# A two-layer graph network on one core: the copy into the accumulator moves to ACT's queue, gathers lose their pacing, and dense rows get a schedule of their own

## The reference

```
h  = relu(layernorm(x))
# stage one (per edge, all its inputs from the node table at dst)
gate  = silu(edge_attr @ W1.T + b1) @ W2.T + b2 + q[type[src], type[dst]]
msg   = gate * h[dst] * cutoff(dist) * node_vec[dst]
agg   = segment_sum(msg, src) / segment_sum(node_vec[dst], src)
x     = x + layernorm(h + agg) * gamma + beta
# stage two
h  = relu(layernorm(x))
m  = (relu(h @ Wr1[rel] + b) @ Wr2[rel])[src] * norm
x  = x + relu(segment_sum(m, dst) + bias2)
```

## Time and profile before

| what | us |
|---|---|
| median of three runs (lowest, highest) | 1523.17 (1517.62, 1532.58) |
| profiled execution, first to last instruction | 1526.4 |
| TensorE, VectorE, ScalarE, GpSimd busy | 1130.4, 1319.3, 668.1, 1026.1 |
| last message of stage one written / last add of stage one issued / first gather of stage two | 687.0 / 740.0 / 743.5 |

### The profile page before, as it was taken

One profiled execution on the slowest core, in us unless ns is written; L12 is line 12 of the kernel. 1 busy time (PEld: TensorE's weight loads), 2 busy tenths in 40 slices (PEclk: granted clock), 3 DMA queues, 4 the chain that ended last, 5 costly groups with the idle time before them and its releaser, 6 DMA issues.

```text
span 1526.4 us, 20418 instructions
## 1 busy us (share of the span) xinstructions
PE 1130.4 (74%) x5198; PEld 831.4 (54%) x5198; DVE 1319.3 (86%) x3932; ACT 668.1 (44%) x1627; POOL 1026.1 (67%) x809
## 2 busy tenths in 40 slices
PE   5889899989999899881068888887878887775000
PEld 2767677777777777771035555555555555554000
DVE  6999999999989998980289999998989899888599
ACT  2444444544445444540155555555555555554000
POOL 7655667777877787566667787877777777766000
PEclk9666655655556655655575656655565556666555
DMA  7999986666666656642445666555555555554899
GB/s 225 307 324 327 328 236 157 153 146 143 142 166 149 149 139 143 155 101 11 100 120 143 166 167 156 140 138 137 136 139 127 132 131 138 138 127 81 328 400 398
DMA packets 154391, 268.73 MB, mean 176 GB/s; under 512 B 73818, under 2 KB 90411, under 8 KB 153380
## 3 DMA queue, kind: packets, MB, share of 16 engines
q1 hardware_dynamic: 78228, 223.53, 43.8%
q0 software_dynamic: 68992, 24.64, 18.5%
q10 hardware_dynamic: 7056, 19.27, 3.1%
HBM read 194.33 MB, written 112.55 MB: 201 GB/s over the span
## 4 chain that ended last, share of the span: by engine, by line
PE 34%; DVE 20%; DMA 19%; POOL 12%; issue 10%; ACT 3%; SPq 1%; POOLq 0%; DVEq 0%; ACTq 0%
PE ps_m L572 10%; POOL agg L485 8%; DMA t<-agg,src_all 6%; PE ps_m L661 6%; PE ps_qs L572 6%; DMA lows<-low 4%; PE ps_k L647 3%; DVE same L858 2%; DMA agg<-y,once 2%; DMA agg<-ysq,once 2%; DVE t L1074 2%; DVE x L1070 2%; PE ps_k L559 2%; PE ps_k L560 2%; PE ps_qs L610 1%
## 5 line engine op out<-in xcount | busy, mean ns | idle before, releaser
L521 POOL DMA_INDIRECT agg<-sums,once x196 | 312.7, 1595 | 103.5 <-issue 79.8
L443 POOL DMA_INDIRECT nodes<-in_table,dst_all x196 | 194.9, 995 | 102.2 <-issue 51.7
L512 POOL DMA_INDIRECT t<-agg,src_all x196 | 191.5, 977 | 66.1 <-issue 53.9
L572 PEld LDWEIGHTS ps_m<-msg,same 128*128 128x128 f32 x980 | 200.8, 314 | 29.0 <-issue 29.0
L572 PE MATMUL ps_m<-msg,same 128*128 128x48 f32 x980 | 208.5, 398 | 1.0 <-issue 1.0
L647 PE MATMUL ps_k<-h_t,rw_sb 56*128 56x256 f32 x588 | 122.7, 536 | 114.0 <-ACT hid L742 91.3
L572 PEld LDWEIGHTS ps_qs<-msg,same 128*128 128x128 f32 x980 | 183.6, 289 | 2.1 <-DVE msg L950 2.1
L572 PE MATMUL ps_qs<-msg,same 128*128 128x49 f32 x980 | 180.7, 363 | 2.0 <-DVE msg L950 2.0
L485 POOL DMA_INDIRECT agg<-x,once x84 | 137.4, 1635 | 43.9 <-issue 21.7
L647 PEld LDWEIGHTS ps_k<-h_t,rw_sb 56*128 56x128 f32 x588 | 62.9, 242 | 157.1 <-ACT hid L742 115.2
L559 PE MATMUL ps_k<-types_lo,low_hot 128*128 128x392 bf16 x196 | 95.7, 488 | 52.7 <-DVE low_hot L833 51.0
(11 more groups left out here) (149 smaller groups left out, 2620.2 us busy)
## 6 DMA issues: line engine op xcount, KB each, us to landing
agg<-in_both SPq DMA_DIRECT2D x14, 2758.0 KB, 15.3
t<-agg SPq DMA_DIRECT2D x49, 784.0 KB, 5.3
kept<-kept_out SPq DMA_DIRECT2D x49, 404.0 KB
kept_in<-kept SPq DMA_DIRECT2D x49, 404.0 KB, 3.5
agg<-bias_rows SPq DMA_DIRECT2D x49, 384.0 KB
out<-t ACTq DMA_DIRECT2D x49, 384.0 KB, 5.8
rows<-in_src_rows SPq DMA_DIRECT2D x49, 256.0 KB, 4.2
rows<-in_dst_rows SPq DMA_DIRECT2D x49, 256.0 KB, 3.2
```

Source lines behind the costliest of these rows:

```text
L443: pool.indirect_dma_start(nodes[s][:, t, :], None, table, bass.IndirectOffsetOnAxis(ap=dst_all[:, c:c + 1], axis=0)).then_inc(nodes_in[b % ...
L512: pool.indirect_dma_start(t2[b % T2S][:, t, :], None, wide, bass.IndirectOffsetOnAxis(ap=src_all[:, c:c + 1], axis=0)).then_inc(ends_in[b ...
L521: pool.indirect_dma_start(agg1, bass.IndirectOffsetOnAxis(ap=once1[b % LAG1][:, t:t + 1], axis=0), sums1[b % LAG1][:, t, :], None, compute ...
L572: last = mm(ps[:, t * width:(t + 1) * width], kept_same[:, at:at + P], m[:, v, :], start=(v == t), stop=(v == TILES - 1))
```

## The change

In stage one: (1) ACT issues all fourteen copies into `agg0` before anything else, as soon as the two index arrays are in. (2) POOL gathers the first 26 blocks with no waits, then waits for the copies; from then on two gathers follow each block's adds, as before. (3) Chunks are taken apart from edge blocks. Blocks 0 to 12 have none; block 13 begins chunks 0 and 1; blocks 14 to 48 each finish one or two (21 with one, 14 with two) and begin the one two ahead. A second chunk of a block stands on VectorE behind the last `type_of`, ahead of the message. (4) The type table holds two types in a number, so a lookup has 196 columns in place of 392 and `type_of` reads 196; two small shift and mask instructions unpack it. (5) The destination's one-hot: VectorE copies four numbers to bf16, TensorE spreads them with four bf16 matmuls of 128 columns, and ScalarE makes the one-hot with Square and Relu. (6) Square roots for edges and chunks are separate. (7) `keep_clock` adds bf16 matmuls of 512 columns whose result nobody reads: nine in a block and one for each chunk.

```diff
-PRERUN = FIRST + 2 * STEPS
+PRERUN = 26
+def dense_steps():
+    steps = [[] for _ in range(NBLOCK)]
+    steps[DENSE0 - 1] = [(None, 0), (None, 1)]
+    c = 0
+    for b in range(DENSE0, NBLOCK):
+        while c * (NBLOCK - DENSE0) < (b + 1 - DENSE0) * NBLOCK:
+            steps[b].append((c, c + 2 if c + 2 < NBLOCK else None))
+            c += 1
...
-                if b < FILLS:
-                    sp.dma_start(fill_to[b], fill_from[b]).then_inc(S["wide_set"], 16)
...
-            for b in range(1, FIRST):
+            for b in range(1, PRERUN):
                 gather(b)
-            for step in range(STEPS):
-                pool.wait_ge(S["onehot_done"], step + 1)
-                gather(FIRST + 2 * step)
-                pool.wait_ge(S["pc_done"], step + 1)
-                gather(FIRST + 2 * step + 1)
             pool.wait_ge(S["wide_set"], 16 * FILLS)
...
+            def keep_clock(ps, n):
+                for _ in range(n):
+                    mm(ps, ident_bf[:, :], spin, start=True, stop=True)
...
             for b in range(NBLOCK):
+                keep_clock(ps_idle, 3)
                 if b + 1 < NBLOCK:
                     lookup(b + 1, 0)
                     lookup(b + 1, 1)
-                pe.wait_ge(S["onehot_done"], b + 1)
-                need(pe, S["onehot_t_done"], b)
+                keep_clock(ps_idle, 1)
+                pe.wait_ge(S["zd_done"], b + 1)
+                need(pe, S["apart_done"], b)
                 for t in range(TILES):
-                    last = nc.tensor.transpose(ps_t[0:NTYPE, t * P:(t + 1) * P], onehot[:, t, :], ident[:, :])
-                last.then_inc(S["turned_t_done"], 1)
+                    last = mm(ps_t[:, t * P:(t + 1) * P], zd_bf[:, t:t + 1].to_broadcast([P, P]), ident_bf[:, :], start=True, stop=True)
+                last.then_inc(S["zd_wide_done"], 1)
...
                 last.then_inc(S["gate_done"], 1)
+                keep_clock(ps_idle, 1)
                 if b + 1 < NBLOCK:
                     h1(b + 1)
-                    centred(b + 1)
+                    keep_clock(ps_idle, 1)
+                for done, begun in steps[b]:
+                    if begun is not None:
+                        centred(begun)
+                        keep_clock(ps_idle, 1)
...
+            act.wait_ge(S["idx_in"], 32)
+            for f in range(FILLS):
+                act.dma_start(fill_to[f], fill_from[f]).then_inc(S["wide_set"], 16)
...
-                nc.scalar.copy(onehot_t[:, :], ps_t[0:NTYPE, :]).then_inc(S["onehot_t_done"], 1)
+                A(apart[:, :], ps_t[0:NTYPE, :], ACT.Square, bias=minus_type[:, :]).then_inc(S["apart_done"], 1)
+                act.wait_ge(S["apart_done"], b + 1)
+                A(onehot_t[:, :], apart[:, :], ACT.Relu, scale=-1.0, bias=1.0).then_inc(S["onehot_t_done"], 1)
...
+                for done, begun in steps[b][1:]:
+                    if begun is not None:
+                        dense_sum(begun)
+                    if done is not None:
+                        dense_var(done)
+                        dense_rsum(done)
+                    if begun is not None:
+                        dense_centre(begun)
+                    if done is not None:
+                        dense_keep(done)
```

More of the change, by code:

```diff
@@ L74, with rooted_at @@
 WIN = place(TILES)
+def dense_steps():
[6 more added lines that the diff above has]
+            c += 1
+    assert c == NBLOCK and max(len(s) for s in steps) == 2
+    return steps
+def rooted_at(steps, b):
+    return [s[0] for s in (steps[b - 1][1:] if b > 0 else []) + (steps[b][0:1] if b < NBLOCK else []) if s[0] is not None]
 def build(nc, table, both, xt_in_dram, xn_in_dram, types, edge_src, edge_dst, src_rows, dst_rows, edge_feat, dist, norm, rel,
@@ L250, in build @@
         ps_c = ps_k[0]
-        ps_l = [ps_k[1][:, a, 0:NHI] for a in range(2)]
+        ps_l = [ps_k[1][:, a, 0:NPK] for a in range(2)]
         ps_h1 = ps_m[0:H, :]
+        ps_idle = ps_k[0][:, 1, :]
         ps_gate = ps_s[:, BE // 2:BE // 2 + TILES * H]
@@ L319, in load_xt, with store_kept @@
                 sp.dma_start(xn[c % 2][:, :], xn_in_dram[c]).then_inc(xn_in[c % 2], 16)
+            def store_kept(b):
+                for c in rooted_at(steps, b):
+                    sp.wait_ge(S["std_d_done"], c + 1)
+                    sp.wait_ge(S["pc_done"], c + 1)
+                    sp.dma_start(kept[c], kept_out[c % 2][:, :]).then_inc(kept_stored[c % 2], 16)
             sp.dma_start(dst_all[:, :], edge_dst).then_inc(S["idx_in"], 16)
@@ L370, in _ @@
                     rows_set += 1
-                sp.wait_ge(S["std_done"], b + 1)
-                sp.wait_ge(S["pc_done"], b + 1)
-                sp.dma_start(kept[b], kept_out[b % 2][:, :]).then_inc(kept_stored[b % 2], 16)
+                if b == DENSE0 - 3:
+                    load_xt(0)
+                    load_xt(1)
+                store_kept(b)
+                for done, begun in steps[b]:
+                    if begun is not None and begun + 2 < NBLOCK:
+                        load_xt(begun + 2)
+            store_kept(NBLOCK)
             sp.wait_ge(kept_stored[0], 16 * uses(NBLOCK - 1, 2))
@@ L708, in _ @@
                 act.wait_ge(S["var_e_done"], b + 1)
-                act.wait_ge(S["var_d_done"], b + 1)
-                need(act, kept_stored[b % 2], 16 * (b // 2))
-                A(kept_out[b % 2][:, PC:PC + G], kept_out[b % 2][:, PC + G:KEPT], ACT.Sqrt, bias=eps[:, :], scale=1.0 / H).then_inc(S["std_done"], 1)
+                need(act, S["rstd_done"], b)
+                A(estd0[:, :], evar0[:, :], ACT.Sqrt, bias=eps[:, :], scale=1.0 / H).then_inc(S["std_done"], 1)
+                for c in rooted_at(steps, b):
+                    root_dense(c)
                 if b + 1 < NBLOCK:
                     gate_hidden(b + 1)
-                    hidden(b + 1)
+                for done, begun in steps[b]:
+                    if begun is not None:
+                        hidden(begun)
+            for c in rooted_at(steps, NBLOCK):
+                root_dense(c)
             sums0_copy(NBLOCK - 1)
@@ L872, in dense_centre, with dense_var, dense_rsum, dense_keep @@
                                        in1=xn[c % 2][:, :].rearrange("p (r f) -> p r f", f=H), op0=ALU.mult, op1=ALU.add).then_inc(S["dc_done"], 1)
-            dense_sum(0)
-            dense_centre(0)
+            def dense_var(c):
+                dve.wait_ge(S["sqd_done"], c + 1)
+                need(dve, kept_stored[c % 2], 16 * (c // 2))
+                V.tensor_reduce(kept_out[c % 2][:, PC + G + TILES:KEPT], sqd[c % 2][:, :, :], AX_X, ALU.add).then_inc(S["var_d_done"], 1)
+            def dense_rsum(c):
+                dve.wait_ge(S["rl_done"], c + 1)
+                V.tensor_reduce(rsum[:, :], rl[c % 2][:, :, :], AX_X, ALU.add).then_inc(S["rsum_done"], 1)
+            def dense_keep(c):
+                dve.wait_ge(S["rsum_done"], c + 1)
+                V.scalar_tensor_tensor(out=kept_out[c % 2][:, 0:PC].rearrange("p (r f) -> p r f", r=NR), in0=cols(rsum[:, :], H),
+                                       scalar=-1.0 / H, in1=rl[c % 2][:, :, :], op0=ALU.mult, op1=ALU.add).then_inc(S["pc_done"], 1)
             for b in range(NBLOCK):
                 s = b % 2
+                done, begun = steps[b][0] if steps[b] else (None, None)
                 at = b * TILES
```

115 lines of the change are left out of this document (72 added, 43 removed).

## The result

The changed kernel takes 1608.84 us (median of four, 1602.99 to 1622.99) where the kernel before takes 1520.39 (four, 1517.41 to 1532.58): a ratio of 1.055 [1.050, 1.061]. It is 88 us slower; 1484 was forecast. The profiled execution took 1614.46 us; its span is 86.3 us above that of the earlier trace rows.

What follows compares the result with a forecast made beforehand. POOL's row of adds was taken to bound stage one: starting at 165 and taking 539 us, it lets stage two begin at 704, 39 sooner. 1526.4 - 39 = 1487, less 3.2 for the median: 1484 us, range 1462 to 1523.

Steps and rivals of the forecast that it cites:

- Start of the compute about 25 us: Stage one's block work begins about 25 us; with the block times it could end at 637, long before 704.
- 25 + 136 + 35 D + 15 > 704: Condition for compute to set stage one's end: 35 blocks of D us each, with D above 15.1.
- Rival 1: Copies hold up ACT at the start, compute starts 100 us late: 1537, or 1550 with SP's loads held too; chance 0.13.
- The start of the adds, 165 (140 to 195): POOL's first add in stage one waits for the later of gathers (140) and copies (156 plus 4 and some): 165 us.
- The adds, 11.1 us a block, 539 in sum: POOL's adds in stage one: 46 blocks with gathers at 11.1 and three at 9.3, 539 us in place of 530.8.
- Blocks without a chunk, 9.7: Stage one's 14 blocks without chunks: VectorE work 8.2 us plus about 1.5 waiting at the reciprocal, 9.7 each.
- Blocks with chunks, 13.6: Stage one's 35 blocks with 49 chunks: VectorE takes 13.1 us plus half a microsecond, 13.6 each.
- the 637 of the prediction: The time at which stage one's compute could end, long before the adds' end at 704.
- The clock, 0.8 in stage one: TensorE's granted clock averages perhaps 0.8 in stage one, against 0.59 to 0.65 before.
- Rival 2: The clock doesn't rise, mean 0.62: TensorE blocks of 12.4 and 15.0, adds end near 742, time 1522; chance 0.15.
- the keepers of the clock and the packed table are worth nothing beyond keeping it off: In stage one, unread matmuls and two-in-one type table only keep compute off the path.
- Second stage untouched: The later stage isn't touched, is charged nothing and takes the same 783 us.

Runs made afterwards that it cites:

- a: The changed kernel with the fourteen copies put back on SP, one at the top of each of its first 14 block iterations: 1503.56 us, ratio 0.983.
- f: The changed kernel with the copies still on ACT, but one at the top of each of its first 14 block iterations: 1503.60 us, ratio 0.989.
- c: The kernel before with only its fourteen copies moved to the start of ACT: 1660.22 us in one run.
- m: The changed kernel with the fourteen copies issued together by ACT only once the constants and the store of `low` have landed: ratio 1.029.
- h: `a` with the copies in 28 halves, three in each of SP's first blocks: 1522.87 us, ratio 1.001.
- e: `a` without the unread matmuls: 1547.18 us, ratio 1.008.
- l: The kernel before with ten unread matmuls of 512 columns added in each block: 1514.25 us, ratio 0.993.
- k: `a` with 33 blocks gathered ahead in place of 26: 1494.24 us, ratio 0.981.
- n: The changed kernel with four copies issued by ACT at the start and ten more one a block: ratio 0.991.

## Why the prediction was wrong

**The step that failed is "Start of the compute about 25 us".** It was given no working: the loads in front of the first block were put at nothing beyond what they took in the trace before, with fourteen copies put beside them. In after the constants landed at 138.3 and ScalarE's first instruction stood at 142.2. `a` and `f` have the first message near 30, after at 157.7, `c` shows the same 122 us in the kernel before, and `m` and the packets show the mechanism. With the compute 120 us late, the prediction's own condition for compute on the path (25 + 136 + 35 D + 15 > 704) is met at once. That step alone doesn't give the whole loss. With blocks as long as predicted, 13 x 9.7 + 35 x 13.6 = 602 us from message 0, stage two would have begun near 157.7 + 602 + 16 = 776; it began at 832.2, and the other 56 us are the mis-sized blocks below, which in after lie on the path.

**Rival 1** named the right resource, DMAs piling up behind outstanding copies. Its main form has the wrong victim (ACT, free at 13.5 us); one clause names SP's loads, the right one. Its price was too small, 1537 to 1550. Its row was the right one: `xt`'s issue took 1.31 us behind one copy. The question to put to that row was not how long the issue is, but how many packets the load has and what each waits for. At 0.13, and out of the range, it was weighted too low.

**The start of the adds, 165 (140 to 195).** After: 187.8, and for another reason than given: the gathers were late (187 and not 140, with the 50 us of waits above), not the copies, which were through by 138. In `a` the add comes at 183.3 after a wait for a copy, inside the ends, which tests the term only in part, since there SP issues the last copy only in its fourteenth block iteration, from which it took 15 us:
```profile
168.03 0.50 SPq L400 DMA_DIRECT2D agg<-in_both  x1
```
The DMA share was 0.95 in 20 to 180 us there, so an earlier issue takes from the loads, as `h` shows. In after the copies had ACT's queue to themselves and took 134 us, near the 121 worked out for copies alone.

**The adds, 11.1 us a block, 539 in sum.** `a`: 721.2 - 183.3 = 537.9. Right, where the compute keeps up. In after from block 15 on it doesn't.

**Blocks without a chunk, 9.7.** 13 of them took 155.3 us in after, 11.9 each. VectorE's own work is 103.6 us in 153, 8.0 a block where 8.2 was predicted. What was mis-sized is the wait at the reciprocal: 43.6 us in 13 waits, 3.4 each and not 1.5. ACT's timeline shows why:
```profile
238.74 0.32 ACT L746 COPY ysq<-ps_qs 128x196 f32<-128x196 f32 x1 [1.31 <-PE ps_qs L617]
239.08 1.28 ACT L771 ACT_TABLE_LOAD   x1
240.38 0.30 ACT L771 ACTIVATE estd<-evar,eps 128x4 f32<-128x4 f32 x1
```
The square root stands on ACT behind the copy of the last block's sums, and so behind `sums0` on TensorE, and behind a table load (`ACT_TABLE_LOAD`, 1.28 us; stage one of the kernel before has as many). With less work on VectorE ahead of it, VectorE is there sooner and waits longer. **Blocks with chunks, 13.6**: 503.4 us for 35, 14.4 each, of them 12.8 VectorE's own work. Together, 13 x 2.25 + 35 x 0.78 = 57 us of compute. In `a` the adds hide nearly all of it: only the last block's add waits for ScalarE's copy of the sums (2.85 us), and message 48 comes at 705.4, not near the 637 of the prediction, held up in its last blocks by gathers that stand behind the adds (waits of 2.1, 4.2 and 8.8 us for `nodes`), as the prediction said.

**The clock, 0.8 in stage one.** 0.84 in 160 to 313 us, 0.73 in 313 to 816. Rival 2 (no rise) did not come true. Its price of 38 us over the forecast is near the 43.6 us by which `e`, which stays at the low level, is slower than `a`; that is luck in part, since rival 2 counts the unread matmuls' own time at the low level and `e` hasn't got them. That "the keepers of the clock and the packed table are worth nothing beyond keeping it off" holds in the main for the keepers: keeping the compute off the path is worth 44 us here, and in `l`, where it was off the path already, they brought 13.5.

**Second stage untouched**: right (780.5 against 783; in `a` 771.9).

With paced copies the sum nearly stands: 1484 is 0.974 of the median of before, `a` measured 0.983, and stage two began at 721 and not 704, which is the adds' later start. That is luck in part: the compute was 57 us longer than forecast, and only the margin between 637 and 704 kept that out of the time.

## What to carry to other kernels

Bulk copies and small loads share the DMA engines packet by packet: a load of many small packets waits one large packet for each of its own when the bulk stands on another queue, so never leave more bulk outstanding than the next load can wait for, and count packets by queue in the first windows of the trace. Before moving DMAs to the start of a kernel, ask what the first compute instruction waits for and how many packets that is. When one engine's row of work sets the end, fill its idle front (`k`), and treat a faster clock elsewhere as worth only what that row waits for it.

## What the runs showed of the hardware that was not expected

- One packet a turn for each queue: 264, 264 and 266 in 30 us, with 35.3 KB against a few hundred bytes in a packet. A copy of 2758 KB is 80 packets of 35 KB, one of 345 KB is 32 of 11 KB: cutting it up shortens the others' turns from 1.8 to 0.63 us.
- ACT took fourteen issues in 9.5 us and 112 in 106.8, 0.95 us each, somewhat faster than they drained (793 of their packets, 32 to a copy, in 30 to 60 us: 1.2 us a copy). SP's issues take 13.1 to 15.2 us each while copies are outstanding on the other queue, in after, `c` (and one of 22.9) and `n`, but under a microsecond in `m` (22 to 25 us); that fewer loads were waiting there by then is a guess. How many packets an engine's queue takes before an issue is held was not settled.
- The granted clock can read 1.00 with TensorE at the low level. In `e` it reads so for all of 100 to 400 us, and in `a` for 40 to 50 us, where the lookup at 44.50 takes 0.37 us. There the duration or spacing of the same lookup has to be read beside it:
```profile
100.00:400.00 300.00, 274.05 (x1171) 227.60 (x1171) 227.45 (x947) 146.92 (x276) 192.36 (x144) 1.00 0.71 185
```
